# State space stage of a four-stage network: convolution per channel piece, two broadcast transfers for l and exp(l), edges computed later, C scaled by VectorE

## Chip, cores and metric

The kernel runs on one core of a Trainium2 chip. The metric is the device time of one execution in microseconds (us). Engines are called by the names of the profile: PE is TensorE, PEld its weight loads, DVE is VectorE, ACT is ScalarE, POOL is GpSimd, SP is the engine that issues the transfers (its queue is SPq).

## The reference, cut to what matters

The program computes six stages on x of shape (4, 1024, 256), float32: a recurrent gated layer, an attention, the gated layer again, a mixture of experts, a state space layer and the mixture of experts again. Only the state space stage (the fifth) is touched by the change:

```
xn = rmsnorm(layernorm(x)) * norm_w                      # x: 4 x 1024 x 256
z, x_ssm, B, C, dt_raw = split(xn @ in_proj_w.T)         # 512, 512, 128, 128, 8 columns
xc = silu(conv_b + sum_k shift(x_ssm, k) * conv_w[:, k]) # 4 taps over time
dt = softplus(dt_raw + dt_bias); dA = exp(-exp(A_log) * dt)
for t in time:                                           # 8 heads of 64 x 128 states
    h = h * dA[t] + dt[t] * xc[t] (outer) B[t]
    y[t] = h . C[t]
out = (y + D * xc) * silu(z) @ out_proj_w.T
x = layernorm(x) + x + out
```

The scan is computed in tiles of 128 time steps. With l the running sum of log dA within a tile, what is inside a tile is a masked product of C and B weighted by exp(l_t - l_s), what comes from earlier tiles is the state H times C * exp(l), and the state is decayed by the exp of the tile's last l (the "edge") once per tile.

## The kernel before, in words

The stage is `ssm_phase`. A group p (of 8) is time tile p of all four batches, so it holds GT = 4 tiles b of 128 x 256 values. Every engine has its own program, and each keeps an order that is written out by hand; semaphores tie them together. In group p an engine does the scan work of group p's tiles b = 0 to 3, and between them the `piece(p + 1, ...)` with number b, which prepares the next group: piece 0 is the split of the normalised input and the unit for dt, piece 1 the units for B, C and the first two channel pieces (f = 0, 1) of x, the softplus, and l; piece 2 the channel pieces f = 2, 3; piece 3 the transposition of B and the product C B (`cb`). A unit is six matmuls of 512 columns (L47).

DVE, in order, in group p (`group`, L1702): `times_dt` of tiles 0 and 1 (L1672, writes `xdt`), then for b = 0 to 3: `weigh(b+1)` (L1666, multiplies the decay matrix `dec` with `cb`), piece 0 (`low`, L1620) if b is 0, `gate(b)` (L1681 four times and L1686, writes `y`), `update_state(b)` (L1692), `times_dt(b+2)`, `residual(b-1)` (L1700), piece 1 or 2; after b = 0 also `statistics(p+2)` (L1605 to L1613). Then piece 3 (L1659), `weigh` of the next group's tile 0, and `residual(3)`. The convolution (`convolve`, L1635) has three taps for DVE, in two halves of two channel pieces; in a half the taps of the two pieces alternate, so that no instruction follows the one that it needs directly. Each half ends with two small copies of the halo (L1639). Half 0 is in piece 1 behind L1648 and L1651, which compute dt and a; half 1 is in piece 2 behind L1655, which starts the edge. The first tap is ACT's (L1498).

ACT, in group p (L1562): Silu of z pieces 0 and 1, Silu of all of `xc` (L1567, it waits for every convolution step of group p), Silu of z pieces 2 and 3, then by b: `hi` (L1546), piece b of the next group, `decays(n + 2)` (eight L1537 and one L1540: the decay matrix of two tiles on), and after b = 2 `normalise(p+2)` (L1554 and L1559). In piece 2 ACT waits between the channel pieces 2 and 3 for the edge of DVE (L1521, L1522). In piece 3 it copies the transposed B (L1527).

POOL (`scale_c`, L1756): per tile it multiplies the broadcast exp(l) with C into `lb[:, slot, :, 1]` (L1762), makes `xd2` (L1770) and decays H (L1776); once a group it does `norms` (L1749 to L1754). SP (`spread`, L1815): stores l and exp(l) of a group as 32 rows to DRAM (L1818) and, per tile, loads the rows of its 8 heads back to all 128 partitions (L1828), 1 MB with l and exp(l) side by side. `lb` has two slots; a transfer waits until ACT has read l and PE has read the scaled C of the tile two before.

PE, in group p (L1443): unit Z3, transposes (`turn_x`, L1409, and `turn_in`, L131), then by b: `tile_y(b)` (L1421 and L1424, 32 matmuls), `tile_out(b-1)` (L1440), `tile_state(b)` (L1432), `turn_x(b+2)`, piece b of the next group. In piece 3 it waits for the edge before it transposes B (L1396), since both lie in one bank of PSUM. Then units Z0, Z1, `tile_out(3)`, Z2.

## Time and profile before

| | |
|---|---|
| median of 3 runs | 2084.59 us (2083.55 to 2085.78) |
| profiled execution | 2082.62 us, of which the span of the instructions is 2080.8 us |
| busy share of the span | PE 85%, DVE 69%, PEld 56%, ACT 54%, POOL 43% |
| state space stage | from about 1415 to 1850 us of the span, 8 groups |
| mean granted TensorE clock | 0.940 of 2.4 GHz |

Times in rows are us from the start of the span; a row of the order of time gives start, duration, engine, line, operation, tiles, shapes and count, and in brackets how long the engine had been idle before it and what released it. The engines are in order, and durations of one instruction include what it waits for inside the engine. One group's stretch, from one `residual(3)` to the next, is read as the period of the stage.

### The profile page before, as it was taken

To read this page: it belongs to the slowest core of one execution; us is meant where nothing else is said; L and a number is where in the kernel's file an instruction comes from. 1 tells how busy PE (TensorE), PEld (TensorE's weight loads), DVE (VectorE), ACT (ScalarE), POOL (GpSimd) and SP (SyncE) were. 2 spreads that over 40 slices of the span, in tenths; PEclk is the share of its full clock that TensorE was granted. 3 is DMA by queue.
4 is the path that set the end of the run, shared out by engine and by line. 5 is a ranking of instruction groups with operands and counts; after the bars stand their busy time and mean duration, and the time that the engine had idled before them with its cause. 6 is when DMAs were issued, how large, how long until landed. Compare 5 with 4: busy or idle time off the path is not lost. (4 is left out here: it accounts for less than half of the span.)

```text
span 2080.8 us, 30681 instructions
## 1 busy us (share of the span) xinstructions
PE 1766.1 (85%) x9600; PEld 1162.4 (56%) x9600; DVE 1433.4 (69%) x2937; ACT 1119.4 (54%) x1592; POOL 904.4 (43%) x601
## 2 busy tenths in 40 slices
PE   4999384899999999986999399995888888869998
PEld 3888263222232323226788377773666666647776
DVE  4545885577777777775445678875877877757886
ACT  2332343899999999983233222215666666522221
POOL 0001321899999999990003321112444444421111
PEclk9999698799999999998999799998899999979999
DMA  4000035525253434300001000001222222210000
GB/s 141 0 0 11 30 121 134 78 42 82 40 74 47 68 53 67 54 1 11 0 0 31 10 16 0 0 0 53 82 83 81 81 81 81 82 41 11 20 20 31
DMA packets 52773, 96.91 MB, mean 47 GB/s; under 512 B 7424, under 2 KB 28896, under 8 KB 48608
## 3 DMA queue, kind: packets, MB, share of 16 engines
q1 hardware_dynamic: 49888, 93.45, 19.4%
q10 hardware_dynamic: 2816, 2.60, 0.6%
q8 instruction: 37, 0.61, 0.1%
q14 instruction: 32, 0.26, 0.0%
HBM read 78.98 MB, written 17.04 MB: 46 GB/s over the span
## 5 line engine op out<-in xcount | busy, mean ns | idle before, releaser
L1152 POOL TENSOR_TENSOR att_weights<-att_weights 128x1024 f32<-128x1024 f32 x288 | 541.1, 1893 | 35.8 <-DVE att_weights L1096 25.0
L1096 DVE SCALAR_TENSOR_TENSOR att_weights<-att_weights,ps 128x512 f32<-128x512 f32 x576 | 370.1, 684 | 170.5 <-ACT att_weights L1071 168.5
L1067 ACT ACTIVATE att_weights<-ps 128x1024 f32<-128x1024 f32 x288 | 294.3, 1022 | 27.9 <-PE ps L1013 23.3
L1071 ACT ACTIVATE att_weights<-att_weights 128x1024 f32<-128x1024 f32 x288 | 302.5, 1051 | 0.0
L679 DVE SCALAR_TENSOR_TENSOR X<-ps,moe_gsel,X 128x256 f32 (+1 forms) x512 | 246.6, 484 | 73.2 <-PE ps L47 57.7
L1027 PE MATMUL ps<-att_weights,att_v_ones 128*32 128x512 f32 (+3 forms) x1536 | 289.4, 498 | 2.6 <-POOL att_weights L1152 2.5
L1010 PE MATMUL ps<-att_q_stack,att_k_stack 128*128 128x512 bf16 (+3 forms) x768 | 232.1, 338 | 69.0 <-DVE att_weights L1096 36.8
L1010 PEld LDWEIGHTS ps<-att_q_stack,att_k_stack 128*128 128x128 bf16 x768 | 74.4, 97 | 321.9 <-DVE att_weights L1096 283.1
L47 PE MATMUL ps<-w_experts_hi,moe_xh 128*128 128x512 f32 x512 | 206.3, 403 | 0.1
L47 PE MATMUL ps<-w_experts_hi,moe_xl 128*128 128x512 f32 x512 | 203.8, 398 | 0.0
L47 PE MATMUL ps<-w_experts_lo,moe_xh 128*128 128x512 f32 x512 | 202.3, 395 | 0.0
L250 ACT ACTIVATE ffn_gates<-ps,ffn_gate_bias 128x512 f32<-128x512 f32 x96 | 66.1, 688 | 211.2 <-PE ps L47 202.6
L728 POOL TENSOR_TENSOR X<-X,moe_bias_sb 128x512 f32 (+1 forms) x32 | 41.5, 1298 | 214.8 <-DVE X L679 213.5
L103 POOL TENSOR_TENSOR ffn_rstd<-ffn_var,ffn_power 128x4 f32<-128x4 f32 x16 | 16.2, 1010 | 273.0 <-DVE ffn_var L116 273.0
L1635 DVE SCALAR_TENSOR_TENSOR ssm_xc<-ssm_xpad,ssm_conv_w,ssm_xc 128x512 f32<-128x512 f32 x96 | 122.1, 1327 | 11.5 <-ACT ssm_xc L1498 11.5
L47 PEld LDWEIGHTS ps<-w_experts_hi,moe_xh 128*128 128x128 f32 x512 | 96.6, 189 | 27.3 <-DVE X L679 3.8
L47 PEld LDWEIGHTS ps<-w_experts_lo,moe_xh 128*128 128x128 f32 x512 | 96.5, 189 | 22.5
L47 PEld LDWEIGHTS ps<-w_experts_hi,moe_xl 128*128 128x128 f32 x512 | 96.7, 189 | 20.7
L1027 PEld LDWEIGHTS ps<-att_weights,att_v_ones 128*32 128x32 f32 x1536 | 56.9, 108 | 90.5 <-issue 54.2
L1537 ACT ACTIVATE ssm_dec<-ssm_lb,ssm_l_tok 128x128 f32<-128x128 f32 x256 | 78.0, 387 | 49.1 <-DMA ssm_lb<-decays 49.1
L1440 PE MATMUL ps<-ssm_out_w,ssm_y 128*128 128x256 f32 x256 | 78.7, 460 | 26.2 <-DVE X L1700 26.2
L594 ACT ACTIVATE moe_gT<-ps 96x512 fp32r<-96x512 f32 x16 | 9.5, 593 | 164.6 <-PE ps L525 164.6
(247 smaller groups left out, 3801.3 us busy)
## 6 DMA issues: line engine op xcount, KB each, us to landing
ssm_lb<-decays SPq DMA_DIRECT2D x32, 1024.0 KB, 4.6
att_q_stack<-qk_parts SPq DMA_DIRECT2D x128, 128.0 KB, 4.8
att_k_stack<-qk_parts SPq DMA_DIRECT2D x120, 128.0 KB, 8.0
qk_parts<-qkv_part SPq DMA_DIRECT2D x32, 384.0 KB, 2.5
out<-X SPq DMA_DIRECT2D x8, 512.0 KB, 2.9
X<-in_x SPq DMA_DIRECT2D x3, 1024.0 KB, 5.3
load_raw<-in_ffn_w SPq DMA_DIRECT2D x8, 256.0 KB, 5.5
ffn_raw<-in_moe_w SPq DMA_DIRECT2D x8, 256.0 KB, 2.7
```

Of the source, the lines that this page charges most:

```text
L47: ins = pe.matmul(out, l(k), r(k), start=first and n == 0, stop=last and n == len(passes) - 1)
L250: act.activation(gates[:, m, gate], ring[:, u % RING], ACT.Tanh if gate == 2 else ACT.Sigmoid, bias=gate_bias[:, gate * KC + m:gate * KC + ...
L679: dve.scalar_tensor_tensor(out=x, in0=ring[:, e // 2, (e % 2) * C:(e % 2 + 1) * C], scalar=gsel[:, s, j, e:e + 1], in1=x, op0=ALU.mult, op ...
L1010: ins = pe.matmul(scores(u)[:, t, c:c + w], SK[:, s, h, kj * P:(kj + 1) * P], SQ[:, s, h, q:q + w], start=True, stop=not diagonal)
L1027: ins = pe.matmul(O(qb)[h * 2 * HD:(h + 1) * 2 * HD, q0:q0 + w], va[:, s, kj, h], Wt[:, u % WU, t, c:c + w], start=kj == 0, stop=m in BLOC ...
L1067: act.activation(Wt[:, u % WU], scores(u), ACT.Exp).then_inc(exp_done, 1)
L1071: act.activation(Wt[:, u % WU], Wt[:, u % WU], ACT.Ln, bias=1.0).then_inc(ln_done, 1)
L1096: dve.scalar_tensor_tensor(out=wt[:, t], in0=wt[:, t], scalar=LIMIT, in1=scores(u)[:, t], op0=ALU.min, op1=ALU.max).then_inc(max_done, 1)
L1152: pool.tensor_tensor(Wt[:, u % WU], Wt[:, u % WU], Wt[:, u % WU], ALU.mult).then_inc(sq_pool, 1)
L1440: ins = pe.matmul(ps_o, y[:, b % 2, k], out_w[:, k], start=k == 0, stop=k == FT - 1)
L1537: ins = act.activation(dec[:, r, h], lb[:, r, h, 0], ACT.Relu, bias=l_tok[:, v, b, h:h + 1], scale=-1.0)
L1635: ins = dve.scalar_tensor_tensor(out=out, in0=src, scalar=conv_w[:, f, k:k + 1], in1=out, op0=ALU.mult, op1=ALU.add)
```

## The change

The convolution is cut into four calls, one for each channel piece, each with its three taps in a row and its halo copy: piece 1 has f = 0, piece 2 has f = 1, piece 3 has f = 2 and 3. l and exp(l) get tiles of their own (`lb` and `rise`), each with a transfer and a semaphore of its own, 512 KB instead of 1 MB, and the store writes them as two planes. The load of l waits only for ACT's reading of the slot, the load of exp(l) only for PE's. ACT computes the edges in piece 3, behind `normalise`, instead of in piece 2. `scale_c` goes from POOL to DVE, behind each `weigh`. DVE's `statistics(p+2)` goes to the group's start, and `residual(3)` ahead of the next group's `weigh`.

```diff
--- before.py
+++ after.py
@@ -1303,7 +1303,7 @@
         a = sb("a", [P, GT, NH])
         l_tok = sb("l_tok", [P, 2, GT, NH])
         l_row = sb("l_row", [GT * NH, 2, P])
-        lb = sb("lb", [P, 2, NH, 2, P])
+        lb, rise = sb("lb", [P, 2, NH, P]), sb("rise", [P, 2, NH, P])
         dec = sb("dec", [P, 2, NH, P])
         edge = sb("edge", [P, 2, 2, GT, NH])
         xdt = sb("xdt", [P, 2, NH, DH])
@@ -1421,7 +1422,7 @@
                         pe.matmul(ps_y[r * DH:(r + 1) * DH, cols], xdt[:, b % 2, 2 * f + r], dec[:, b % 2, 2 * f + r],
                                   start=True, stop=False)
                     for r in range(2):
-                        ins = pe.matmul(ps_y[r * DH:(r + 1) * DH, cols], H[:, b, 2 * f + r], lb[:, b % 2, 2 * f + r, 1],
+                        ins = pe.matmul(ps_y[r * DH:(r + 1) * DH, cols], H[:, b, 2 * f + r], rise[:, b % 2, 2 * f + r],
                                         start=False, stop=True)
                 ins.then_inc(y_summed, 1)
 
@@ -1517,11 +1518,11 @@
                     act.activation(l_tok[:, v], ps_dt, ACT.Copy).then_inc(l_copied, 1)
                 if b == 2:
                     unit(p, v, U_X + 2)
+                    unit(p, v, U_X + 3)
+                if b == 3:
                     act.wait_ge(edge_in, p + 1)
                     act.activation(edge[:, v, 0], edge[:, v, 0], ACT.Exp)
                     act.activation(edge[:, v, 1], ps_last, ACT.Exp).then_inc(edge_done, 1)
-                    unit(p, v, U_X + 3)
-                if b == 3:
                     act.wait_ge(b_turned, p + 1)
                     act.wait_ge(state_done, p * GT)
                     act.activation(b_tm[:, :, :], ps_b, ACT.Copy).then_inc(b_copied, 1)
@@ -1534,7 +1535,7 @@
                 if not isinstance(n, int) or n > 1:
                     act.wait_ge(y_summed, n - 1)
                 for h in range(NH):
-                    ins = act.activation(dec[:, r, h], lb[:, r, h, 0], ACT.Relu, bias=l_tok[:, v, b, h:h + 1], scale=-1.0)
+                    ins = act.activation(dec[:, r, h], lb[:, r, h], ACT.Relu, bias=l_tok[:, v, b, h:h + 1], scale=-1.0)
                 ins.then_inc(dsub_done, 1)
                 act.wait_ge(dsub_done, n + 1)
                 act.activation(dec[:, r], dec[:, r], ACT.Exp, scale=-1.0).then_inc(dexp_done, 1)
@@ -1601,6 +1602,8 @@
         def _(dve):
             def statistics(p):
 
+                if not isinstance(p, int) or p:
+                    dve.wait_ge(shift_done, p)
                 for b in range(GT):
                     dve.bn_stats(norm.stats[:, 0, b], tile_of(p, b))
                 dve.drain()
@@ -1621,22 +1624,16 @@
                                                    in1=f32(norm.xh[:, 0, k]), op0=ALU.mult, op1=ALU.subtract)
                 ins.then_inc(norm.xl_done, 1)
 
-            def convolve(p, v, half):
-
-                base = (p * FT + 2 * half) * (TAPS - 1)
+            def convolve(p, v, f):
+
+                base = (p * FT + f) * (TAPS - 1)
+                dve.wait_ge(tap_done, p * FT + f + 1)
                 for k in range(1, TAPS):
-                    for n in range(2):
-                        f = 2 * half + n
-                        out, src = xc[:, v, f], xpad[:, f, :, k:k + P]
-                        if k == 1:
-                            dve.wait_ge(tap_done, p * FT + f + 1)
-                        else:
-                            dve.wait_ge(conv_step, base + 2 * (k - 2) + n + 1)
-                        ins = dve.scalar_tensor_tensor(out=out, in0=src, scalar=conv_w[:, f, k:k + 1], in1=out,
-                                                       op0=ALU.mult, op1=ALU.add)
-                        ins.then_inc(conv_step, 1)
-                for f in (2 * half, 2 * half + 1):
-                    dve.tensor_copy(xpad[:, f, :, 0:TAPS - 1], xpad[:, f, :, P:P + TAPS - 1]).then_inc(halo_done, 1)
+                    if k > 1:
+                        dve.wait_ge(conv_step, base + k - 1)
+                    dve.scalar_tensor_tensor(out=xc[:, v, f], in0=xpad[:, f, :, k:k + P], scalar=conv_w[:, f, k:k + 1],
+                                             in1=xc[:, v, f], op0=ALU.mult, op1=ALU.add).then_inc(conv_step, 1)
+                dve.tensor_copy(xpad[:, f, :, 0:TAPS - 1], xpad[:, f, :, P:P + TAPS - 1]).then_inc(halo_done, 1)
 
             def piece(p, v, b):
                 if b == 0:
@@ -1655,6 +1652,8 @@
                     dve.tensor_tensor(edge[:, v, 0], ps_last, l_tok[:, v], ALU.subtract).then_inc(edge_in, 1)
                     convolve(p, v, 1)
                 if b == 3:
+                    convolve(p, v, 2)
+                    convolve(p, v, 3)
                     dve.wait_ge(cb_done, p + 1)
                     dve.tensor_tensor(cb[:, v], ps_cb, tri[:, :].unsqueeze(1).broadcast_to([P, GT, P]), ALU.mult)\
                         .then_inc(cbm_done, 1)
@@ -1665,6 +1664,12 @@
                 dve.wait_ge(cbm_done, p + 1)
                 dve.tensor_tensor(dec[:, b % 2], dec[:, b % 2], cb[:, v, b].unsqueeze(1).broadcast_to([P, NH, P]),
                                   ALU.mult).then_inc(w_done, 1)
+
+            def scale_c(p, v, b):
+
+                dve.wait_ge(rise_in[b % 2], (p * (GT // 2) + b // 2 + 1) * 16)
+                dve.tensor_tensor(rise[:, b % 2], rise[:, b % 2], cT[:, v, b].unsqueeze(1).broadcast_to([P, NH, P]),
+                                  ALU.mult).then_inc(cts_done, 1)
 
             def times_dt(p, v, b):
                 n = p * GT + b
@@ -1700,11 +1705,14 @@
                 dve.tensor_tensor(x, x, ps_o, ALU.add).then_inc(x_done, 1)
 
             def group(p, v, left):
+                if left == 2:
+                    statistics(p + 2)
                 times_dt(p, v, 0)
                 times_dt(p, v, 1)
                 for b in range(GT):
                     if b + 1 < GT:
                         weigh(p, v, b + 1)
+                        scale_c(p, v, b + 1)
                     if left and b == 0:
                         piece(p + 1, 1 - v, 0)
                     gate(p, v, b)
@@ -1715,12 +1723,12 @@
                         residual(p, b - 1)
                     if left and b in (1, 2):
                         piece(p + 1, 1 - v, b)
-                    if left == 2 and b == NORM_AT:
-                        statistics(p + 2)
                 if left:
                     piece(p + 1, 1 - v, 3)
+                residual(p, GT - 1)
+                if left:
                     weigh(p + 1, 1 - v, 0)
-                residual(p, GT - 1)
+                    scale_c(p + 1, 1 - v, 0)
 
             dve.memset(H[:, :, :, :], 0.0).then_inc(h_done, GT)
             for f in range(FT):
@@ -1731,11 +1739,11 @@
             dve.wait_ge(init_done, 1)
             dve.tensor_scalar(neg_a[:, :], neg_a[:, :], -1.0, None, ALU.mult).then_inc(init_done, 3)
             dve.wait_ge(init_done, 4)
-            dve.wait_ge(shift_done, 1)
             statistics(1)
             for b in range(GT):
                 piece(0, 0, b)
             weigh(0, 0, 0)
+            scale_c(0, 0, 0)
             groups(dve, group)
             dve.wait_ge(x_done, FREE + TILES)
 
@@ -1752,15 +1760,6 @@
                 pool.wait_ge(minus_done, p + 1)
                 pool.tensor_tensor(shifts[:, :, :], scales[:, :, :], minus[:, :].unsqueeze(1).broadcast_to([P, 2, GT]), ALU.mult)
                 pool.tensor_scalar(grow[:, :], scales[:, 0], 1.0, None, ALU.add).then_inc(shift_done, 1)
-
-            def scale_c(p, n, v, b):
-
-                pool.wait_ge(lb_in[b % 2], (p * (GT // 2) + b // 2 + 1) * 16)
-                if not isinstance(n, int) or n:
-                    pool.wait_ge(y_summed, n - 1)
-                rise = lb[:, b % 2, :, 1]
-                pool.tensor_tensor(rise, rise, cT[:, v, b].unsqueeze(1).broadcast_to([P, NH, P]),
-                                   ALU.mult).then_inc(cts_done, 1)
 
             def scale_x(p, v, n, b):
 
@@ -1786,8 +1785,6 @@
                         norms(p + 2)
                     if b + 1 < GT:
                         decay_state(v, n + 1, b + 1)
-                    if left or b + AHEAD < GT:
-                        scale_c(p + (b + AHEAD) // GT, n + AHEAD, v if b + AHEAD < GT else 1 - v, (b + AHEAD) % GT)
                 if left:
                     scale_x(p + 1, 1 - v, n + 1, 0)
 
@@ -1795,8 +1792,6 @@
             pool.wait_ge(powers_set, 1)
             norms(0)
             norms(1)
-            scale_c(0, 0, 0, 0)
-            scale_c(0, 1, 0, 1)
             scale_x(0, 0, 0, 0)
             groups(pool, group)
 
@@ -1815,18 +1810,19 @@
             def spread(p, v):
 
                 sp.wait_ge(l_copied, 2 * (p + 1))
-                sp.dma_start(decay_dram[v], l_row[:, :, :]).then_inc(l_stored, 16)
+                sp.dma_start(decay_dram[v].rearrange("k r t -> r k t"), l_row[:, :, :]).then_inc(l_stored, 16)
                 sp.wait_ge(l_stored, 16 * (p + 1))
                 for b in range(GT):
                     n = p * GT + b
 
-                    if isinstance(p, int) and p == 0 and b < 2:
-                        pass
-                    else:
+                    free = not (isinstance(p, int) and p == 0 and b < 2)
+                    rows = slice(b * NH, (b + 1) * NH)
+                    if free:
                         sp.wait_ge(dsub_done, n - 1)
+                    sp.dma_start(lb[:, b % 2], decay_dram[v, 0, rows].partition_broadcast(P)).then_inc(lb_in[b % 2], 16)
+                    if free:
                         sp.wait_ge(y_summed, n - 1)
-                    sp.dma_start(lb[:, b % 2], decay_dram[v, b * NH:(b + 1) * NH].partition_broadcast(P))\
-                        .then_inc(lb_in[b % 2], 16)
+                    sp.dma_start(rise[:, b % 2], decay_dram[v, 1, rows].partition_broadcast(P)).then_inc(rise_in[b % 2], 16)
 
             spread(0, 0)
             with sp.Fori(0, PT // 2 - 1) as i:
@@ -1853,7 +1849,7 @@
         ident16 = sb("ident16", [P, P], BF16)
         proj_bias = sb("proj_bias", [P, C], F32)
         parts_dram = nc.dram_tensor("qk_parts", (2, PARTS, B * C, T), BF16).ap()
-        decay_dram = nc.dram_tensor("decays", (2, GT * NH, 2, P), F32).ap()
+        decay_dram = nc.dram_tensor("decays", (2, 2, GT * NH, P), F32).ap()
         ps = ctx.enter_context(nc.psum_tensor("ps", [P, 8, BANK], F32))
```

## Rows read from the trace of the kernel before

**Rows 1.** One line's instructions (L1659, once a group): duration and first and last start.
```profile
L1659 DVE TENSOR_TENSOR ssm_cb<-ps,ssm_tri x8: 678/684/685, 1453.5 to 1811.5; 128x512 f32<-128x512 f32 x8
```
**Rows 2.** Busy time of each engine (us, instructions), granted clock, DMA, in two stretches.
```profile
1610.30:1661.90 51.60, 43.74 (x282) 33.43 (x281) 41.81 (x69) 34.69 (x73) 22.42 (x16) 0.93 0.22 82
...
1606.74:1610.30 3.56, 3.56 (x9) 2.89 (x10) 1.68 (x2) 3.55 (x4) 0.00 (x0) 0.55 0.00 0
```
**Rows 3.** DVE in order of time, one group (1610 to 1662 us).
```profile
1615.58 0.69 DVE L1672 TENSOR_TENSOR ssm_xdt<-ps,ssm_dt 128x512 f32<-128x512 f32 x1 [1.25 <-PE ps L1409]
1616.18 1.22 DVE L1666 TENSOR_TENSOR ssm_dec<-ssm_dec,ssm_cb 128x1024 f32<-128x1024 f32 x1
1617.32 1.40 DVE L1620 SCALAR_TENSOR_TENSOR w_even_lo<-ps,ssm_norm_w,w_even_hi 128x512 fp32r<-128x512 f32 x2
...
1619.89 0.69 DVE L1686 TENSOR_TENSOR ssm_y<-ssm_y,ssm_zs 128x512 f32<-128x512 f32 x1
...
1621.70 1.39 DVE L1605 BATCH_NORM_STATS2 ssm_stats<-X 128x6 f32 x4
...
1628.27 2.92 DVE L1686 TENSOR_TENSOR ssm_y<-ssm_y,ssm_zs 128x512 f32<-128x512 f32 x1
...
1632.85 0.19 DVE L1651 TENSOR_TENSOR ssm_a<-ssm_dt,ssm_neg_a 128x32 f32<-128x32 f32 x1
1632.98 4.85 DVE L1635 SCALAR_TENSOR_TENSOR ssm_xc<-ssm_xpad,ssm_conv_w,ssm_xc 128x512 f32<-128x512 f32 x6
1637.75 2.42 DVE L1639 COPY ssm_xpad<-ssm_xpad 128x12 f32<-128x12 f32 x2
...
1646.66 8.49 DVE L1635 SCALAR_TENSOR_TENSOR ssm_xc<-ssm_xpad,ssm_conv_w,ssm_xc 128x512 f32<-128x512 f32 x5 [1.06 <-ACT ssm_xc L1498]
```
**Rows 4.** POOL in order of time, the same group.
```profile
1628.26 2.39 POOL L1762 TENSOR_TENSOR ssm_lb<-ssm_lb,ssm_cT 128x1024 f32<-128x1024 f32 x1
...
1647.31 1.04 POOL L1776 TENSOR_TENSOR ssm_H<-ssm_H,ssm_edge 128x512 f32<-128x512 f32 x1 [6.23 <-PE ps L1424]
1648.31 2.82 POOL L1762 TENSOR_TENSOR ssm_lb<-ssm_lb,ssm_cT 128x1024 f32<-128x1024 f32 x1
```
**Rows 5.** PE in order of time, the same group.
```profile
1622.62 1.99 PE L1440 MATMUL ps<-ssm_out_w,ssm_y 128*128 128x256 f32 x8
...
1634.00 0.44 PE L1421 MATMUL ps<-ssm_dec,ssm_xdt 128*64 128x128 f32 x4
...
1641.15 0.40 PE L47 MATMUL ps<-w_even_lo,w_even_hi 128*128 128x512 f32 x1
...
1650.28 0.60 PE L1396 MATMUL ps<-ident,ssm_bT 128*128 128x128 f32 x4
...
1654.16 0.40 PE L47 MATMUL ps<-w_even_lo,w_even_hi 128*128 128x512 f32 x1
1658.14 3.60 PE L1440 MATMUL ps<-ssm_out_w,ssm_y 128*128 128x256 f32 x8 [3.58 <-DVE X L1700]
```
**Rows 6.** ACT in order of time, the same group.
```profile
1622.36 2.44 ACT L1537 ACTIVATE ssm_dec<-ssm_lb,ssm_l_tok 128x128 f32<-128x128 f32 x8 [5.96 <-DMA ssm_lb<-decays]
...
1646.54 2.43 ACT L1537 ACTIVATE ssm_dec<-ssm_lb,ssm_l_tok 128x128 f32<-128x128 f32 x8
...
1649.96 2.06 ACT L1554 ACTIVATE ssm_xn<-X,ssm_shifts,ssm_scales 128x256 f32 x4
...
1653.90 0.57 ACT L1527 ACTIVATE ssm_b_tm<-ps 128x512 f32<-128x512 f32 x1
```
**Rows 7.** DMA issues, 1450 to 1800 us: count, size, median us to landing.
```profile
ssm_lb<-decays SPq DMA_DIRECT2D x27, 1024.0 KB, 4.6
decays<-ssm_l_row SPq DMA_DIRECT2D x7, 32.0 KB, 1.5
```
**Rows 8.** DVE in order of time, the last group.
```profile
1830.30 1.25 DVE L1666 TENSOR_TENSOR ssm_dec<-ssm_dec,ssm_cb 128x1024 f32<-128x1024 f32 x1 [5.19 <-ACT ssm_dec L1540]
...
1838.33 2.78 DVE L1686 TENSOR_TENSOR ssm_y<-ssm_y,ssm_zs 128x512 f32<-128x512 f32 x1
```

More of the change, by code:

```diff
@@ L1332, in ssm_phase @@
         lb_in = [sem(f"lb_in{r}") for r in range(2)]
+        rise_in = [sem(f"rise_in{r}") for r in range(2)]
         (dsub_done, edge_in, dexp_done, edge_done, w_done, cts_done, x_turned, xdt_done, xd2_done, y_summed,
```

## The prediction

> **What bounds the kernel now.** The profile's page comes first: no engine is near full over the whole span, so the question is the stage. Line L1659 runs once a group and gives the period: 1811.5 - 1453.5 = 358.0 us over 7 groups, 51.1 us each [rows 1]. The busy times of one such period come second: PE 43.7, DVE 41.8, ACT 34.7, POOL 22.4 of 51.6 us [rows 2]. None is full, so a ring of dependences through several engines sets the period, and a saving counts only where that ring passes. The order of time on DVE, POOL, PE and ACT gives the ring. I start it where DVE ends the second `times_dt`, at 1615.58 + 0.69 = 1616.27, called 0 below.
>
> In that order the reader is to see three things. First, DVE instructions stretch when POOL multiplies. L1686 takes 0.69 us at one place and 2.92 at another, beside a POOL L1762 that starts 0.01 us earlier and takes 2.39 [rows 3, 4]. The two halo copies take 2.42 us, and five convolution steps take 8.49 us, where six free ones take 4.85, 0.81 each [rows 3]. The excess is 2.2 + 2.2 + (8.49 - 4.04 = 4.4) = 8.9 us a group, of which the L1776 of POOL that the five steps also meet has at most its 1.0 [rows 4]; `scale_c` costs DVE about 8 us a group. Second, ACT waits 5.96 us for the transfer of l [rows 6]. Third, PE stands 3.58 us for `residual(2)` ahead of `tile_out(3)`, because that residual lies behind the second half of the convolution, and when it goes on it has a low clock: eight L1440 take 3.60 us, elsewhere 1.99 [rows 5]; the granted clock of one such stretch is 0.55, against 0.93 over the group, so it lies mostly at 1.2 instead of 2.4 GHz [rows 2].
>
> **The change part by part, along the ring.**
>
> *C by VectorE.* L1762 leaves POOL (2.39 to 2.82 us each [rows 4]) and the same shape goes to DVE behind each L1666. The trace of before doesn't show it there; the nearest row is L1666 itself, also 128 x 1024 with two SBUF inputs: 1.22 us alone, 1617.32 - 1616.18 = 1.14 from start to start [rows 3]. So 4 x 1.14 = 4.6 us a group are added and some 8 us of stalls are removed: DVE's load falls by 3.4 us. But `scale_c(1)` lies ahead of `low` and `gate(0)`, and PE's `tile_y(1)` takes up directly behind that gate's L1686 (the end, 1620.58, is 4.31 after 0). That point moves to 5.45: the ring gets 1.14 longer there.
>
> *From there to dt.* In before, a (L1651) ends at 1633.04, 12.46 us later. Of the 2.2 us that the stretched L1686 lost, none or all may have reached L1651; since it also waits for ACT's Ln, which comes at about that time, I take 0.6. So 11.9: a ends at 17.3. PE's l products and then `tile_y(2)` follow 1634.00 - 1633.04 = 0.96 later, at 18.3 [rows 3, 5].
>
> *Convolution in four.* One step alone behind the one that it needs is not in the trace. From below it is 0.81 (steps that alternate); from above I take 0.12 more, the overlap of neighbours that a dependent one loses (L1666 ends 0.08 after its successor's start, and a gap of 0.04 [rows 3]). I take 2.4 + 0.15 us for a channel piece. Between the first piece (done at 19.9) and `weigh(3)` DVE now waits for the decay matrix of ACT, whose order behind l is as before: 18.3 + 0.6 for three small copies + 2.44 + 1.06 = 22.4, say 22.5. The moved half stands behind `residual(2)`, so PE's 3.58 us wait is gone. From 22.5 DVE has `weigh`, `scale_c`, `gate(2)`, two small ones, the edge, piece f = 1, `gate(3)`, two small ones, f = 2 and 3 and L1659: 1.14 + 1.14 + 1.8 + 1.0 + 2.5 + 1.8 + 1.0 + 5.0 + 0.7 = 16.1 (a gate is 1.8 since the 4.31 hold one, a `weigh` of 1.14 and a `low` of 1.4), and two collisions with the POOL multiplications that stay (1.04 each [rows 4]), 18.2: it is at 40.7. The Trainium skill's page "VectorE: DVE Perf Modes", section "Rules for kernel authors", says that a chain on this engine should be judged by the count of its operations, since the pipeline drains anyway. By it the dependent steps would cost nothing extra and DVE would be there at 39.8. The row of the alternating steps can't decide it, and the ring below doesn't hang on it.
>
> *Edges later.* ACT no longer waits for DVE between channel pieces 2 and 3, but the edge now stands behind `decays` and `normalise`, and PE's piece 3 waits for it. PE ends unit X3 at 1641.55, 7.55 after the start of `tile_y(2)` [rows 5]; ACT copies it and does its tap in some 1.6; then `decays` (1649.96 - 1646.54 = 3.42), `normalise` (1653.90 - 1649.96 = 3.94) [rows 6] and two small exps, 0.3. Sum 18.3 + 7.55 + 1.6 + 3.4 + 3.9 + 0.3 = 35.0 for the edge. PE would otherwise be there about 32.3 (`tile_y(3)` at 22.5 + 1.14 + 1.04 + 1.14 + 1.8 + 0.1 = 27.7; 1.8 for it, 1.99 for `tile_out(2)`, 0.8 for `tile_state(3)`), so a wait of about 2.7 us takes the place of the 3.58. Behind PE's waiting L1396 are cb, Z0, Z1 and `tile_out(3)`: to the end of Z1 it is 1654.56 - 1650.28 = 4.3, then 1.99 [rows 5]: 41.3. DVE is there at 40.7, just ahead.
>
> *The end of the ring.* `residual(3)` 0.4, `weigh` 1.14, `scale_c` 1.14, and `statistics`, which is moved here and took from 1621.70 on some 2.05 (four L1605, 1.39, and six small ones) [rows 3]: 46.1. In before the statistics lay where DVE then waited for ACT. Now they delay `times_dt(0)`: by ACT's and PE's order `turn_x(0)` would be ready at 35.0 + 0.6 (L1396) + 0.6 (L1527) + 3.4 (`decays`) + some 5 for the Silus and the transposes = 44.6. `times_dt(0)`, `turn_x(1)`, `times_dt(1)` take 0.7 + 0.7 + 0.7: the period is 48.2. If PE's clock falls after the wait for the edge, 3.60 - 1.99 = 1.6 us more [rows 5]: 49.8. I take 48.9, between them, and 2.2 us saved a group. Six periods give 13.2 us.
>
> *Two transfers.* l is loaded as soon as ACT has read the slot, so ACT's wait of 5.96 us in tile 2 goes [rows 6]; in the full groups the time is hidden, since DVE then waits for dt in any case. A 512 KB transfer isn't in the trace; it lies between the 1.5 us of 32 KB and the 4.6 us of 1 MB [rows 7]. exp(l) of tile 2 is issued when `tile_y(0)` is done, at 1.2, so by 5.8 at the latest, and DVE asks for it at 7.8. On SP's queue the next l waits behind it, and is needed later still. At nothing, then, inside the ring; in the prologue ACT waits 0.9 us for the first 1 MB, so 0 to 0.9 us are saved there, and I take 0.4. By the page "DMA: Bandwidth & Descriptors" of the Trainium skill, section "Anatomy of one DMA" (some 2.0 us fixed and the bytes over 436 GB/s, told there for the GpSimd path), an estimate for 512 KB is 3.2 us; the prologue would then save the whole 0.9.
>
> *The group before the last* has no statistics and no `normalise`: the edge is there 3.9 us earlier, so DVE's 40.7 decides, and without 2.05 the period is some 46.5: 4.6 us saved.
>
> *The last group* has nothing beside the scan. DVE waited 5.19 us there for the decay matrix of tile 2, which waited for its transfer, and one L1686 took 2.78 [rows 8]. `weigh(2)` can start about 4 us earlier, L1686 gets back 2.1, and two `scale_c` in the path cost 2.3: 3.9 us, with one collision either way 3 to 5. I take 4.
>
> Sum: 13.2 + 4.6 + 4 + 0.4 = 22.2 us. The profiled execution took 2082.62 us (span 2080.8 and 1.8 around it), the median is 2.0 us above it: 2060.4 and 2.0, so 2062.4; I say 2062.
>
> **The rivals.** (a) *The convolution's chain becomes the bound.* It was 0.6 us ahead of PE's `tile_out(3)`. If dependent steps and collisions cost 2 us more a group, that is all of the steady saving, and the ends of the stage remain: 2084.6 - 8.6 = 2076; with 3 us more it is no change. For it: all of DVE's slack is used up. Against it: the collisions would have to be twice those counted.
>
> (b) *Slower: the stalls move instead of going.* The place is DVE's `scale_c` and `weigh`, back to back, with POOL's L1770 and L1776 asked for at that time. There are eight of these a group at 1.04 us, and my sum has two of them. If all eight hold DVE in the ring, it is 6.2 us more: 6 x (6.2 - 2.2) = 24 slower in the steady groups, less some 4 at the ends: 2105. It decides from 2.2 + 9.0 / 6 = 3.7 us, that is from four such collisions more. For it speaks that the stretched steps show an instruction waiting for the whole of another [rows 3, 4]; against it, that most of them fall where DVE waits anyway or reads PSUM. The Trainium skill's page "SBUF — State Buffer", section "SBUF: two separate sides", calls the port pair of the two engines an exclusive lock, also for a DVE operation with two SBUF inputs; by that rule `scale_c` on DVE is an operation that takes it, four times a group, and the trace agrees (2.92 against 0.69).
>
> (c) *The moved parts cost nothing.* If the clock holds and the statistics end ahead of `turn_x`, the period is 46.6: 6 x 4.5 + 9 = 36 faster, 2049. Against it: the statistics wait for `residual(3)` by the order of DVE.
>
> (d) *The change does nothing*, since l's transfer was hidden and PE's wait for `residual(2)` is only exchanged for the wait for the edge, with the low clock: steady period 51, 2084.6 - 6 = 2078 to 2084.
>
> **How the numbers follow.** Chances: forecast 0.62, (a) 0.10, (b) 0.12, (c) 0.08, (d) 0.08. The forecast's own range is 2053 to 2075, by periods of 48.2 less 0.5 to 50.6 and ends of 5 to 11. With (c) and the near parts of (a) and (d) the range is 2049 to 2080. What a measurement of this kernel can tell from no change is 0.2%, 4.2 us: faster is below 2080.4, which takes the forecast, (c), most of (a) and half of (d): 0.81. Same gets 0.09, slower 0.10, nearly all of it (b).
>
> **What would show it.** L1659 or L1567 once every 48 to 50 us. The stretched L1686 and L1639 are gone, and stretches of over 2 us on DVE are rare. PE waits 2 to 4 us ahead of L1396 for ACT's edge, and no longer for `residual(2)`. ACT has no wait for lb in tile 2. DVE idles ahead of `weigh(3)` and during piece 1, and `times_dt(0)` starts directly behind the statistics. The prediction is wrong if DVE's stretches stay near 9 us a group, or if PE's wait for the edge is over 5 us.

## The result and the profile after

| | median | stage span |
|---|---|---|
| before | 2084.07 us (4 runs) | 410.2 us |
| after | 2056.03 us (2055.1 to 2058.89, 4 runs) | 383.2 us |
| ratio | 0.9867 (0.9852 to 0.9883) | 27.0 us less |

The change makes the kernel 1.3% faster; 2062 us was forecast, in a range of 2049 to 2080. "Stage span" is from the first instruction that computes a (L1651 before, L1648 after, 1439.1 and 1439.0 us) to the start of the last residual; it leaves out what other stages vary by from run to run, some 4 us, and is used for all kernels below, each from one profile.

One line's instructions after (the mask of C B, once a group): duration, first and last start, beside [rows 1].
```profile
L1658 DVE TENSOR_TENSOR ssm_cb<-ps,ssm_tri x8: 682/683/683, 1448.4 to 1790.5; 128x512 f32<-128x512 f32 x8
```
That is 48.9 us a group against 51.1. From one group's second `times_dt` to the next one's the seven periods after are 49.87, 47.95, 48.02, 47.95, 48.01, 48.36 and 43.73 us; before they are 51.2 to 51.4 six times, and 50.71. Now DVE in order of time after, one group, beside [rows 3].
```profile
1607.15 0.69 DVE L1677 TENSOR_TENSOR ssm_xdt<-ps,ssm_dt 128x512 f32<-128x512 f32 x1 [0.75 <-PE ps L1410]
1607.76 1.22 DVE L1665 TENSOR_TENSOR ssm_dec<-ssm_dec,ssm_cb 128x1024 f32<-128x1024 f32 x1
1608.89 1.22 DVE L1671 TENSOR_TENSOR ssm_rise<-ssm_rise,ssm_cT 128x1024 f32<-128x1024 f32 x1
...
1612.60 0.69 DVE L1691 TENSOR_TENSOR ssm_y<-ssm_y,ssm_zs 128x512 f32<-128x512 f32 x1
...
1615.54 2.07 DVE L1671 TENSOR_TENSOR ssm_rise<-ssm_rise,ssm_cT 128x1024 f32<-128x1024 f32 x1
...
1618.68 1.27 DVE L1691 TENSOR_TENSOR ssm_y<-ssm_y,ssm_zs 128x512 f32<-128x512 f32 x1
...
1624.73 0.19 DVE L1645 SCALAR_TENSOR_TENSOR ssm_dt<-ssm_dta,ps 128x32 f32<-128x32 f32 x1 [3.26 <-ACT ssm_dta L1512]
1624.95 0.19 DVE L1648 TENSOR_TENSOR ssm_a<-ssm_dt,ssm_neg_a 128x32 f32<-128x32 f32 x1
...
1630.24 1.23 DVE L1665 TENSOR_TENSOR ssm_dec<-ssm_dec,ssm_cb 128x1024 f32<-128x1024 f32 x1 [2.76 <-ACT ssm_dec L1541]
1631.38 2.07 DVE L1671 TENSOR_TENSOR ssm_rise<-ssm_rise,ssm_cT 128x1024 f32<-128x1024 f32 x1
...
1636.16 2.98 DVE L1634 SCALAR_TENSOR_TENSOR ssm_xc<-ssm_xpad,ssm_conv_w,ssm_xc 128x512 f32<-128x512 f32 x3
...
1641.82 2.32 DVE L1634 SCALAR_TENSOR_TENSOR ssm_xc<-ssm_xpad,ssm_conv_w,ssm_xc 128x512 f32<-128x512 f32 x3
1644.06 0.17 DVE L1636 COPY ssm_xpad<-ssm_xpad 128x12 f32<-128x12 f32 x1
1644.13 2.32 DVE L1634 SCALAR_TENSOR_TENSOR ssm_xc<-ssm_xpad,ssm_conv_w,ssm_xc 128x512 f32<-128x512 f32 x3
...
1646.45 0.68 DVE L1658 TENSOR_TENSOR ssm_cb<-ps,ssm_tri 128x512 f32<-128x512 f32 x1
1649.03 0.42 DVE L1705 TENSOR_TENSOR X<-X,ps 128x256 f32 x1 [1.89 <-PE ps L1441]
```
With 0 at 1607.15 + 0.69 = 1607.84, the reader can lay these rows beside the prediction's ring: the first gate ends at 5.45, a at 17.30, and the next group's second `times_dt` (1655.10) ends at 47.95. DVE now has waits of 3.26 and 2.76 us, and stands 1.89 us for `tile_out(3)`. The stretches of 2.2 to 4.4 us are gone. Four short ones stay, each beside one of POOL's L1769 or L1775: L1671 takes 2.07 instead of 1.22 us twice, one L1691 takes 1.27 instead of 0.69, and the three steps of f = 1 take 2.98 instead of 2.32. That is 2.9 us a group, where the kernel before lost 8.9.

PE in order of time after, the same group, beside [rows 5].
```profile
1635.36 0.44 PE L1422 MATMUL ps<-ssm_dec,ssm_xdt 128*64 128x128 f32 x4 [1.72 <-DVE ssm_y L1691]
...
1642.82 0.66 PE L1397 MATMUL ps<-ident,ssm_bT 128*128 128x128 f32 x4 [2.71 <-ACT ssm_edge L1525]
...
1646.99 1.89 PE L1441 MATMUL ps<-ssm_out_w,ssm_y 128*128 128x256 f32 x8
```
ACT in order of time after, the same group, beside [rows 6].
```profile
1609.14 2.45 ACT L1538 ACTIVATE ssm_dec<-ssm_lb,ssm_l_tok 128x128 f32<-128x128 f32 x8 [1.86 <-PE ps L1425]
...
1638.54 2.06 ACT L1555 ACTIVATE ssm_xn<-X,ssm_shifts,ssm_scales 128x256 f32 x4
...
1642.59 0.18 ACT L1525 ACTIVATE ssm_edge<-ps 128x32 f32<-128x32 f32 x1
```
The wait for `residual(2)` (3.58 us) has become one of 2.71 for the edge, and `tile_out(3)` takes 1.89 us where it took 3.60. Whether the clock falls behind the new wait is read from the stretch that follows it, since `tile_out(3)` comes later. In the group shown, that stretch takes 1646.99 - 1642.82 = 4.17 us up to `tile_out(3)`. Busy time, clock and DMA after, behind the same wait in two other groups; the first row ends where `tile_out(3)` begins, the second goes on through it:
```profile
1496.98:1502.74 5.76, 5.76 (x24) 4.99 (x25) 4.21 (x8) 5.02 (x11) 0.00 (x0) 0.70 0.00 0
...
1594.78:1600.90 6.12, 6.12 (x33) 5.35 (x34) 4.23 (x8) 5.36 (x12) 0.00 (x0) 1.00 0.00 0
```
The six full groups all have this wait, of 2.69 to 2.71 us. Behind four of them the granted clock stays at 1.00 (the 2.4 GHz level) and PE is at `tile_out(3)` in 4.17 or 4.18 us. Behind the first and the sixth it is 0.70, that is, PE runs part of the stretch at 1.2 GHz, and PE is there 1.6 us later. In before, the eight L1440 behind the wait of 3.5 to 3.6 us were slow in every group (0.55 in the second of [rows 2]).

### The profile page after: what moved, and what is told of

It reads as the page before. It is cut to its first block and busy times, and to the rows that moved or that the text cites. A ratio compares the mean times of both kernels' runs of the same rounds, so it can differ in the third digit from the quotient of the medians.

```text
span 2053.3 us, 30656 instructions
## 1 busy us (share of the span) xinstructions
PE 1747.4 (85%) x9600; PEld 1147.1 (56%) x9600; DVE 1420.6 (69%) x2969; ACT 1119.9 (55%) x1592; POOL 817.0 (40%) x569
## 5 line engine op out<-in xcount | busy, mean ns | idle before, releaser
L1769 POOL TENSOR_TENSOR ssm_xd<-ssm_xdt,ssm_edge 128x512 f32<-128x512 f32 x32 | 35.5, 1109 | 169.2 <-DVE ssm_xdt L1677 139.9
L1013 PE MATMUL ps<-ident,neg 128*128 128x128 bf16 x512 | 95.3, 221 | 0.0
L1775 POOL TENSOR_TENSOR ssm_H<-ssm_H,ssm_edge 128x512 f32<-128x512 f32 x32 | 41.6, 1300 | 127.6 <-PE ps L1425 127.6
```

Of the source, the lines that this page charges most:

```text
L1013: ins = pe.matmul(scores(u)[:, t, c:c + P], neg[:, :], ident16[:, :], start=False, stop=True)
L1775: pool.tensor_tensor(H[:, b], H[:, b], edge[:, v, 1, b].unsqueeze(2).broadcast_to([P, NH, DH]), ALU.mult).then_inc(h_decayed, 1)
```

## The experiments

All twelve were timed in three rounds beside the kernel before. "C" is the multiplication of C by exp(l). What they say together is in the table; stage span of the kernel before is 410.2 us.

| kernel | median us | ratio to before (95%) | stage span |
|---|---|---|---|
| after, C by POOL | 2050.98 | 0.9838 (0.9821 to 0.9854) | 375.9 |
| after, edges early | 2070.16 | 0.992 (0.9904 to 0.9937) | 393.3 |
| after, one transfer | 2064.50 | 0.9898 (0.9882 to 0.9915) | 389.7 |
| after, statistics back | 2053.07 | 0.9842 (0.9825 to 0.9858) | 381.0 |
| before, C by DVE | 2068.97 | 0.9917 (0.9901 to 0.9934) | 394.4 |
| before, two transfers | 2077.29 | 0.9961 (0.9949 to 0.9973) | 405.5 |
| before, convolution in four | 2056.90 | 0.986 (0.9844 to 0.9877) | 383.7 |
| before, edges late | 2060.78 | 0.9888 (0.9871 to 0.9904) | 386.4 |
| before, both of these and residual(3) early | 2054.60 | 0.9849 (0.9826 to 0.9871) | 380.3 |
| after, edges ahead of normalise | 2048.03 | 0.982 (0.9798 to 0.9842) | 371.7 |
| the same, C by POOL | 2043.68 | 0.9801 (0.9785 to 0.9818) | 369.2 |
| the same, statistics ahead of piece 1 | 2039.74 | 0.9781 (0.9758 to 0.9804) | 365.8 |

**C back on POOL.**
```diff
-                        scale_c(p, v, b + 1)          # DVE, behind each weigh
+                    if left or b + AHEAD < GT:        # POOL, behind decay_state
+                        scale_c(p + (b + AHEAD) // GT, v if b + AHEAD < GT else 1 - v, (b + AHEAD) % GT)
```


> The changed kernel with one part undone: POOL multiplies C with exp(l) again. Theory of the stalls: DVE loses 4 x 1.14 us a group but gets back stretches of some 8 us a group, part of them in the convolution of f = 1, 2, 3, which has under 2 us of slack; the period goes from 48.0 to between 49 and 51 us, the time from 2056 to 2062 to 2076. Rival, that the stalls lay off the ring and C on DVE only costs its 1.14 us ahead of the first gate: the period falls to about 47, the time to 2045 to 2052.

The rival was right: 7.3 us less in the stage. DVE in order of time in this kernel, one group:
```profile
1604.36 0.69 DVE L1671 TENSOR_TENSOR ssm_xdt<-ps,ssm_dt 128x512 f32<-128x512 f32 x1 [0.86 <-PE ps L1410]
...
1608.67 0.69 DVE L1685 TENSOR_TENSOR ssm_y<-ssm_y,ssm_zs 128x512 f32<-128x512 f32 x1
...
1626.31 2.36 DVE L1665 TENSOR_TENSOR ssm_dec<-ssm_dec,ssm_cb 128x1024 f32<-128x1024 f32 x1 [2.76 <-ACT ssm_dec L1541]
...
1634.28 2.31 DVE L1636 COPY ssm_xpad<-ssm_xpad 128x12 f32<-128x12 f32 x1
...
1637.65 1.77 DVE L1685 TENSOR_TENSOR ssm_y<-ssm_y,ssm_zs 128x512 f32<-128x512 f32 x1
...
1646.70 0.42 DVE L1699 TENSOR_TENSOR X<-X,ps 128x256 f32 x1 [1.12 <-PE ps L1441]
```
The stretches are back, on L1665, L1636 and L1685, 1.1 + 2.1 + 1.1 = 4.3 us. But DVE still waits 1.12 us for PE at the end, so they lie in slack, while the first gate ends 4.31 after 0 instead of 5.45. All stretches of this group come to 5.0 us, against 2.9 with C on DVE. PE's wait for the edge is 3.54 us here, and behind it the granted clock is 0.59 to 0.72 in five of six groups. In the one group where it stays at 1.00 the period is 46.21, 1.74 us under the changed kernel's 47.95; the other five take 47.2 to 48.3, so the lower clock eats a part of the gain. By parts the 7.3 us are 6.4 in the six periods and 1.8 in the last group, less 1.0 lost in the group before the last. Once the convolution is out of the way, C on DVE is a loss.

**Edges early again.**
```diff
                     unit(p, v, U_X + 2)
+                    act.wait_ge(edge_in, p + 1)      # and the two Exps of the edge
                     unit(p, v, U_X + 3)
```


> The changed kernel with the edges computed by ACT between the channel pieces f = 2 and 3 again. Theory: PE's wait of 2.7 us ahead of the transposition of B goes, but ACT waits some 2.4 us for DVE's edge in their place, and ACT's chain (decays, normalise, decays, Silu) is as close to setting the period as PE's: 1 to 2 us a group slower, 2062 to 2070. Rival, that the later edges are a loss hidden in the change, since PE waits for them in the ring: 1 to 2 us a group faster, 2043 to 2051.

As the theory had it, 10.1 us more. Waits in this kernel, 1500 to 1750 us: us in total, times, longest.
```profile
PE ps L47 <- ACT ssm_zs L1495: 19.1, 5, 3.8
...
ACT ssm_edge L1522 <- DVE ssm_edge L1652: 12.4, 5, 2.5
```
ACT loses 2.5 us a group to DVE's edge, and its late Silu makes PE wait 3.8 us for the bank of unit Z2.

**Statistics back behind the third times_dt.**
```diff
-                if left == 2:                         # at the start of group
-                    statistics(p + 2)
+                    if left == 2 and b == NORM_AT:    # behind residual(b - 1)
+                        statistics(p + 2)
```


> The changed kernel with the statistics of the group after the next back behind the third times_dt. Theory: DVE waits there 3.3 us for dt in any case, so they cost nothing, and the first times_dt of a group, which starts directly behind them now, comes 1.2 us earlier; the second one is then held by PE's turn_in, so the period falls by some 0.5 us: 2052 to 2055. Rival, that their move filled a gap and is a part of the gain: 2060 to 2068.

The time is in the theory's range, and the stage is 2.2 us shorter, though the intervals of the two kernels overlap. The periods are 48.51, 48.54, 48.24, 47.34, 48.24 and 47.20 us. Their differences go with the clock: behind PE's wait for the edge, again 2.7 us long, the granted clock is 0.70 to 0.75 in the first, second, third and fifth, and 1.00 in the other two. At the higher clock a period with the statistics here is 47.34 against 47.95 us, so the 0.5 us that the theory asked for are there, and four groups at the lower clock instead of two hide most of them. The rival, that their move was a part of the gain, is refuted.

**C by DVE alone, on the kernel before.**
```diff
                         weigh(p, v, b + 1)
+                        scale_c(p, v, b + 1)          # on lb[:, b % 2, :, 1], off POOL
```


> The kernel before with one part alone: DVE multiplies C with exp(l). Theory of the stalls: DVE is in the ring of that kernel from the first convolution half to residual(2); it gets back some 8 us of stretches for 4.6 us of work, one of them ahead of the ring's start, and the period falls from 51.3 by 2 to 3 us: 2063 to 2071. Rival, that the convolution in four and the later edges bring the gain: 2080 to 2090.

15.8 us less in the stage: six periods of 49.5 us in the mean (1.8 less each), and 5.0 less in the group before the last. The stretches were in the ring of that kernel, and taking them away helps. The sign of this one edit depends on where the convolution lies.

**Convolution in four, edges late and residual(3) ahead of weigh; nothing else.**
```diff
-                    convolve(p, v, 1)                 # piece 2: f = 2 and 3
+                    convolve(p, v, 1)                 # f = 1; piece 3 has f = 2 and 3
+                    # ACT: the edge in piece 3; DVE: residual(GT - 1) ahead of weigh
```


> The kernel before with one part alone: the convolution in four, the edges behind normalise, residual(3) ahead of weigh; POOL scales C, one transfer, statistics where they were. If this part carries the gain and C on DVE costs some 6 us once it is there, as the run with C back on POOL suggests, the period is about 47.5 and only the last group keeps its waits for the transfer: 2053 to 2062. If instead the gain needs C off POOL or the transfers apart, 2072 or more.

29.9 us less, more than the whole change, so this part carries the gain. What `residual(3)` ahead of `weigh` gives of it was not tried by itself.

**Two transfers alone.**
```diff
+                    sp.dma_start(lb[:, b % 2], decay_dram[v, 0, rows].partition_broadcast(P))
+                    sp.dma_start(rise[:, b % 2], decay_dram[v, 1, rows].partition_broadcast(P))
```


> The kernel before with one part alone: l and exp(l) in two transfers. ACT's wait of 6 us in tile 2 goes, but the next thing that counts in a full group is DVE's wait for dt, or its full load behind it; the gain is 0 to 0.6 us a group and some 3 us in the last group: 2078 to 2083. If the transfer of l is in the ring, 2 us a group: 2066 to 2072.

4.7 us less in the stage. The mask's row goes from 1453.1 to 1812.4, 51.3 us a group, no shorter than before; from the last mask to the last residual it is 33.7 instead of 37.8 us. The gain is in the last group. The median is 0.7 us below the expected range; the first expectation had the mechanism right.

**One transfer, in the changed kernel.**
```diff
-        lb, rise = sb("lb", [P, 2, NH, P]), sb("rise", [P, 2, NH, P])
+        lb = sb("lb", [P, 2, NH, 2, P])
```


> The changed kernel with one transfer for l and exp(l) again. In the full groups DVE waits 3.3 us for dt anyway, so that a later weigh(2) costs up to 1 us a group; the last group waits for its transfer again, some 2 to 4 us: 2058 to 2066. If the transfers' overlap is all hidden: 2055 to 2058.

6.5 us more in the stage, 4.8 of them behind the last mask (36.5 against 31.7). Most of the rest is one period of 49.61 where the change has 48.01 us: the granted clock is 0.70 behind its wait for the edge, 1.00 in the change. Other stages added 4.2. Two second `times_dt` (1611.64 and 1659.61) are 47.97 us apart, as in the change: in a steady group the overlap is hidden. DVE in order of time in this kernel:
```profile
1621.88 1.23 DVE L1664 TENSOR_TENSOR ssm_dec<-ssm_dec,ssm_cb 128x1024 f32<-128x1024 f32 x1 [2.91 <-ACT ssm_dec L1540]
...
1629.23 0.19 DVE L1644 SCALAR_TENSOR_TENSOR ssm_dt<-ssm_dta,ps 128x32 f32<-128x32 f32 x1 [0.86 <-ACT ssm_dta L1511]
```
The wait of 2.91 us ahead of `weigh(2)` is paid out of the one ahead of dt, 0.86 instead of 3.26.

**Convolution in four alone, edges late alone.** Each is its own edit of the two above, on the kernel before.
```diff
-            def convolve(p, v, half):
+            def convolve(p, v, f):                    # 0 | 1 | 2, 3 in pieces 1, 2, 3
```


> The kernel before with the convolution in four alone: the edges stay between the channel pieces 2 and 3, residual(3) stays behind weigh. PE no longer waits for residual(2), but ACT still waits some 3 us for DVE's edge, as in the run with the edges early again, and its Silu then holds the group: period 49 to 50.5, 2066 to 2078. If the convolution carries the gain by itself: below 2060.


```diff
                     unit(p, v, U_X + 3)
                 if b == 3:
+                    act.wait_ge(edge_in, p + 1)       # moved from between U_X + 2 and U_X + 3
```


> The kernel before with the edges behind normalise alone. ACT's wait of 3 to 4 us for DVE's edge goes, but half 1 of the convolution still lies ahead of residual(2) and PE waits for that: only DVE's wait of 1.1 us for the tap is saved: 2076 to 2081. If the edges carry the gain by themselves: below 2065.

Both expectations were missed by 9 us or more, and in both runs the alternative stated last came true: either alone brings most of it (26.5 and 23.8 us), and together 29.9. PE in order of time with the edges late alone, then DVE:
```profile
1646.33 1.97 PE L1440 MATMUL ps<-ssm_out_w,ssm_y 128*128 128x256 f32 x8 [2.49 <-DVE X L1700]
```
```profile
1634.15 6.94 DVE L1635 SCALAR_TENSOR_TENSOR ssm_xc<-ssm_xpad,ssm_conv_w,ssm_xc 128x512 f32<-128x512 f32 x6
1641.01 2.49 DVE L1639 COPY ssm_xpad<-ssm_xpad 128x12 f32<-128x12 f32 x2
```
DVE no longer waits 1.06 us for the tap, so the half ends 1.1 us earlier; I had counted that. I had not counted that PE's wait then is 2.49 us and that the eight L1440 behind it take 1.97 instead of 3.60. The eight L1440 take 1.97 us in every group of this kernel, and 3.3 to 3.65 in every full group before. The 1.1 us came with 1.6 of clock. Together they are the saving of the group shown, 51.3 to 48.6 (1604.93 to 1653.49). The six periods are 47.4 to 48.6, 47.9 in the mean; where the other 0.7 us come from was not traced. With the convolution alone, PE waits 1.6 to 2.0 us for `residual(2)`, and ACT's wait for the edge is 1.63 instead of 3.3, since DVE reaches the edge earlier.

**Edges ahead of normalise.** The prediction's ring says what holds the changed kernel: `normalise`, 3.9 us, ahead of the edge that PE waits for.
```diff
                         decays(n + AHEAD, ...)
+                    if left and b == 2:
+                        edges(p + 1, 1 - v)           # out of piece 3
                     if left == 2 and b == SCALE_AT:
                         normalise(p + 2)
```


> The changed kernel with ACT's edges moved ahead of normalise and behind decays. If PE's wait of 2.7 us for the edge is in the ring, residual(3) comes 1.9 us earlier (then DVE's own convolution holds it) and with the Silu of xc close behind the period falls by some 1.1 us: 2046 to 2051. If DVE's or ACT's chain sets the period by itself, no change from 2056 (2054 to 2058).

11.5 us less in the stage. PE no longer waits for the edge in the full groups, and the six periods are 46.3 to 46.5 us: 1.5 less than a period of the change at the higher clock, and 3.4 and 2.0 less than its first and sixth, which lose 1.6 us to the lower clock. So the theory holds, and the edge's wait also carried the clock's cost.

**The same with C on POOL, and with the statistics ahead of piece 1.**
```diff
-        NORM_AT, SCALE_AT = 0, 2
+        NORM_AT, SCALE_AT = 1, 2                      # and statistics(p + 2) ahead of piece(p + 1, 1 - v, 1)
```


> The changed kernel with C scaled by POOL and the edges ahead of normalise, the statistics left at the group's start. Against the best version this shows what the statistics' place is worth once the edge is out of the ring: if they then hold the first times_dt by some 1 us a group, 2043 to 2048; if not, 2038 to 2042.

> The changed kernel with C scaled by POOL again, the edges ahead of normalise and the statistics ahead of piece 1, with POOL's norms a tile later. If the three savings add: period 45.5 to 46.5, 2038 to 2045. If with C on POOL the stretched DVE instructions hold residual(3), so that the earlier edge gives nothing: as the run with C on POOL alone, 2049 to 2053.

Both came as expected: 369.2 and 365.8 us in the stage, periods of 46.2 and 45.4, and 2039.74 us at the best, 2.2% under the kernel before. DVE in order of time in the best version:
```profile
1640.35 0.68 DVE L1665 TENSOR_TENSOR ssm_cb<-ps,ssm_tri 128x512 f32<-128x512 f32 x1
1640.95 0.41 DVE L1706 TENSOR_TENSOR X<-X,ps 128x256 f32 x1
1641.28 1.22 DVE L1672 TENSOR_TENSOR ssm_dec<-ssm_dec,ssm_cb 128x1024 f32<-128x1024 f32 x1
1643.24 0.69 DVE L1678 TENSOR_TENSOR ssm_xdt<-ps,ssm_dt 128x512 f32<-128x512 f32 x1 [0.74 <-PE ps L1410]
```
`residual(3)` follows the mask with no wait, and the first `times_dt` waits for `turn_x(0)`, not for the statistics. The period is 1645.08 - 1599.74 = 45.3 us.

## Why the prediction was right, step by step

- *The ring up to the edge.* Forecast and measured, in us after 0: first gate 5.45 and 5.45, a 17.3 and 17.30, `tile_y(2)` 18.3 and 18.25 (1626.09), the edge 35.0 and 34.93, PE's wait 2.7 and 2.71, the end of `tile_out(3)` 41.3 and 41.04. These points were worked out from rows of before alone.
- *The end of the ring and the low clock.* The forecast gave 48.2 us a group if the clock holds and 49.8 if it falls behind PE's wait for the edge, and took 48.9. Both came: 47.95 to 48.02 in the four groups at the higher clock, and 49.87 in the first, which ran at 0.70 behind the wait. The sixth was at 0.70 too and took 48.36, since the group behind it has no statistics at its start; the sum of six equal periods left that out. The mis-sized term is the 0.8 us for the clock: it was half of 1.6 in every group, and two groups of six lost 1.6, 0.5 in the mean. No run shows what decides between the two, so this term could be given only as a chance.
- *The base.* 51.1 us a group before is the mean from mask to mask, with a short first one of 50.5 in it; the six periods compared here are 51.3. So six periods gave 17.7 us (from 1461.61 to 1769.44, now 1461.31 to 1751.47), not 13.2: 1.2 from the base and 3.3 from the periods after.
- *Convolution steps in a row.* Three take 2.32 us, and 2.31 with the copy from start to start: 0.75 to 0.77 each, no dearer than alternating ones. The 0.12 for a dependent step was wrong. It is also missing from the prediction's own sum, where 2.5 us for a piece is three times 0.81 and a copy, so leaving it out would not give the 39.8 named there. What the Trainium skill's page "VectorE: DVE Perf Modes", section "Rules for kernel authors", says of chains, that only the number of operations counts, agrees with the trace. The mask ended at 39.3, not 40.7: 0.6 of it is the pieces, and 0.6 that the two collisions took 0.85 and 0.66 us instead of 1.04 each.
- *The group before the last* gave 7.0 us (50.71 to 43.73), forecast 4.6. DVE's chain held it, as forecast, and ended its mask at 39.0; and the terms of the forecast (40.7 + 0.4 + 1.14 + 1.14 + 2.1) give 45.5, not 46.5.
- *The last group* gave 2.2 us (29.14 to 26.97 from the second `times_dt` to the last residual), forecast 4. Two transfers alone gave 4.0 there (25.13), so the transfers were sized rightly, and C on DVE takes 1.8 back, since with C on POOL in the changed kernel it is 25.13 too. DVE in order of time after, beside [rows 8]:
```profile
1799.22 1.38 DVE L1691 TENSOR_TENSOR ssm_y<-ssm_y,ssm_zs 128x512 f32<-128x512 f32 x1
...
1809.90 2.06 DVE L1671 TENSOR_TENSOR ssm_rise<-ssm_rise,ssm_cT 128x1024 f32<-128x1024 f32 x1
```
 Two collisions, 0.7 and 0.8 us, and a third of 0.3, where one was allowed for.
- *The prologue* gave 0.3 us. Sum: 17.7 + 7.0 + 2.2 + 0.3 = 27.2, against 22.2.
- *C by DVE.* The text gave it 4.6 us for 8 us of stalls, and the ring charged it 1.14 us at the gate and 1.14 behind `residual(3)`. What it didn't do is ask for the time with C left on POOL. The run says some 7 us less: C on DVE removes stalls that the split convolution had already put into slack. Of the 2.28 us charged, 1.74 show at equal clock. So the total came near the forecast although this part, counted with the others in place, is a loss.
- *Rival (b)*, stalls that move: they did, in small: the four stretches of 2.9 us in all [DVE after, above], and none is ahead of the first gate. *Rival (a)* didn't come, since DVE had 1.89 us left. *Rival (d)*, that the wait for the edge brings the low clock with it, came true in two groups of six.

DMA issues after, 1450 to 1750 us, beside [rows 7].
```profile
ssm_rise<-decays SPq DMA_DIRECT2D x24, 512.0 KB, 3.9
ssm_lb<-decays SPq DMA_DIRECT2D x24, 512.0 KB, 4.7
```
512 KB take 3.9 us, and 4.7 where it is issued some 0.4 us behind the other, as much as 1 MB took before. The estimate of 3.2 us worked out from the Trainium skill's page "DMA: Bandwidth & Descriptors", section "Anatomy of one DMA", was too short for this queue; the measurement decides.

## What to carry to other kernels

Two edits that lie in one ring don't add: here either the convolution's split or the later edge brought some 24 to 26 us, both 30. (The run with both also had `residual(3)` early.) An edit can be a gain alone and a loss beside the others, as C on VectorE was (-16 us alone, +7 in the whole, +2.5 once the edges lie ahead of normalise), so price each edit once with the others in place. A stage span from one profile carries a chance part: one group more at the lower clock is 1 to 2 us, so before a difference of 2 or 3 us is given to an edit, count the groups at each clock. A walk along the ring from the rows of before, with every engine's order kept, placed the new kernel's points within 0.3 us up to the edge, and also named the next thing to move.

## What the runs showed of the hardware

- The length of PE's wait alone doesn't decide whether its clock falls. In the changed kernel six waits of 2.69 to 2.71 us were followed by a granted clock of 1.00 four times and 0.70 twice, and in the run with the statistics back by 1.00 twice and 0.70 to 0.75 four times. Waits of 3.5 us had 1.00 behind them once in C back on POOL (1545.43) and once in the run with convolution, edges and `residual(3)` (1545.99), and a wait of 1.99 us had 0.69 behind it in the convolution alone (1695.29). The fall cost 1.3 to 1.6 us over the matmuls up to `tile_out(3)` (5.5 to 5.8 instead of 4.17 us), once 2.6 (C back on POOL, 0.59).
- A VectorE multiplication of 1.22 us with two SBUF inputs took 2.07 beside a GpSimd one of 512 elements, and 2.36 beside one of 1024 (C back on POOL, where a halo copy of 0.17 us took 2.31 too). The four GpSimd multiplications of C stretched VectorE's instructions by some 8 us a group in the kernel before, and taking them off GpSimd saved the stage 15.8 us; in the changed kernel putting them back saved it 7.3.
- The first group after the prologue took 49.87 us where the later ones take 47.95: 1.6 of the 1.92 us are the lower clock behind its wait for the edge; the other 0.3 isn't traced.
